# A decoder layer on one core: the order of steps on all five engines replaced, 19 products of zeros fewer

## The reference

```python
x = x + attn(layernorm(x), Wqkv, Wo)       # 16 heads of 16, rope, causal softmax
x = x + xattn(layernorm(x), ctx, ~mask)    # softmax(x @ ctx.T / 16) @ ctx, masked
x = x + ffn(layernorm(x), ...)
# ffn: probs = softmax(x @ gate_w.T); the 2 best of 8 experts, weights not renormalised
#      every expert is computed: h_e = silu(x @ w1_e.T) * (x @ w2_e.T), 176 wide
#      y = sum_e comb_e * (h_e @ w3_e.T) + the same form with a shared part, 352 wide
```

## Time and profile before

| what | value |
|---|---|
| median of 3 runs | 284.23 us (284.11 to 285.96) |
| the profiled execution's own time | 284.33 us |
| its span, from first to last instruction | 282.7 us |
| granted TensorE clock, mean | 0.998 |
| busy share of the span | PE 95%, PEld 75%, ACT 61%, DVE 59%, POOL 42% |

### The profile page before, as it was taken

How to read it: one execution, slowest core, us unless ns; L and a number is a source line. 1 busy time by engine, 2 the same in 40 slices (tenths; PEclk the granted TensorE clock), 3 DMA queues, 4 the chain that set the end, 5 groups by cost and what they waited for, 6 DMA issues and landing times.

```text
span 282.7 us, 4951 instructions
## 1 busy us (share of the span) xinstructions
PE 267.5 (95%) x1834; PEld 212.2 (75%) x1844; DVE 166.5 (59%) x361; ACT 172.6 (61%) x288; POOL 120.1 (42%) x133
## 2 busy tenths in 40 slices
...
GB/s 231 371 378 9 0 3 5 0 4 0 2 0 4 75 5 260 0 5 74 2 3 113 253 42 3 1 3 0 0 2 16 58 175 227 10 2 1 0 0 77
DMA packets 11879, 17.09 MB, mean 60 GB/s; under 512 B 1904, under 2 KB 8272, under 8 KB 11856
## 3 DMA queue, kind: packets, MB, share of 16 engines
...
...
## 4 chain that ended last, share of the span: by engine, by line
PE 69%; ACT 9%; POOL 9%; DMA 5%; issue 3%; DVE 2%; SPq 1%; DVEq 0%; ACTq 0%; POOLq 0%
PE bank L758 28%; PE bank L866 14%; PE bank L771 8%; PE bank L812 3%; PE bank L765 3%; DMA gate_raw<-gate 3%; PE bank L798 2%; PE bank L919 2%; POOL prob_lo L392 2%; DMA q_t<-negm_t 2%; PE bank L836 2%; POOL w_lo L399 2%; PE bank L791 2%; PE bank L816 2%; ACT q_t L493 2%
## 5 line engine op out<-in xcount | busy, mean ns | idle before, releaser
L392 POOL TENSOR_TENSOR prob_lo<-prob,prob_hi 128x1536 f16<-128x1536 f32 x16 | 49.7, 3118 | 22.7 <-ACT prob_hi L512 22.6
L758 PE MATMUL bank<-x_hi,w_hi 128*128 128x512 f32 x112 | 45.5, 407 | 0.3 <-ACT prob L505 0.3
L758 PE MATMUL bank<-x_hi,w_lo 128*128 128x512 f32 x112 | 44.2, 395 | 0.0
L758 PE MATMUL bank<-x_lo,w_hi 128*128 128x512 f32 x112 | 44.0, 393 | 0.0
L549 ACT CAST h_hi<-h_c 128x512 fp32r<-128x512 f32 x28 | 17.3, 620 | 41.8 <-DVE h_c L735 23.2
L726 DVE TENSOR_TENSOR h_c<-bank,h_s 128x512 f32<-128x512 f32 x28 | 19.3, 690 | 31.2 <-PE bank L758 21.6
L583 DVE TENSOR_REDUCE negm<-bank 128x2 f32<-128x512 f32 (+1 forms) x48 | 31.2, 684 | 6.8 <-PE bank L793 3.9
L866 PE MATMUL bank<-w_hi,h_hi 128*128 128x256 f32 x112 | 32.5, 290 | 0.1
L740 DVE TENSOR_TENSOR h_lo<-h_c,h_hi 128x512 fp32r<-128x512 f32 x28 | 20.2, 728 | 19.5 <-ACT h_hi L549 19.5
L866 PE MATMUL bank<-w_lo,h_hi 128*128 128x256 f32 x112 | 31.7, 283 | 0.0
L866 PE MATMUL bank<-w_hi,h_lo 128*128 128x256 f32 x112 | 31.6, 283 | 0.0
...
## 6 DMA issues: line engine op xcount, KB each, us to landing
...
```

The source lines that it names most:

```text
L392: eng.tensor_tensor(prob_lo[:, b % 2], prob[:, b % 2], prob_hi[:, b % 2], ALU.subtract)\
L758: ins = pe.matmul(dst, a(k), c(k), start=(k == 0 and i == 0), stop=(k == kt - 1 and i == 2))
```

## The change

The five lists of `ORDER` are replaced. SP, POOL, ACT and DVE keep exactly their steps (16, 73, 228 and 200) in another order. PE keeps its steps too, but for the products of zeros: `early` falls from 33 to 14, `late` stays at 19. Nothing else in the file changes; a blank line goes, so that the lines of the new kernel are one lower. The head and the tail of the lists, and the middle where `up.0` begins:

```diff
     "SP": """
-        ln1.0 mt.0 mt.1 mt.2 ro.0 w3.0 ct.0 mt.3 ro.1 ct.1 cb.0 ct.2 y.0 ct.3 cb.1 y.1
+        ln1.0 mt.0 mt.1 mt.2 w3.0 ct.0 mt.3 ro.0 ct.1 cb.0 ct.2 ro.1 ct.3 cb.1 y.0 y.1
     "POOL": """
-        ln1.0 ln1.1 tr.7 qk.0 ln1.2 sh.0 qk.1 ln1.3 w12.0 sh.1 w12.1 w12.2 w12.3 w12.4 w12.5 w12.6 qk.2 sh.2 qk.3
+        ln1.0 ln1.1 qk.0 sh.0 tr.7 qk.1 sh.1 ln1.2 w12.0 qk.2 sh.2 w12.1 qk.3 sh.3 qk.4 ln1.3 h.0 h.1 sh.4 h.2 qk.5
...
     "ACT": """
...
-        s.41 h.13 s.42 s.43 s.44 ln3n.1 t3.1 s.45 s.46 h.14 lg.1 s.47 h.15 up.0 ct.1 ot.2 dn.0 up.1 dn.1 w3.0 w3.1
+        w12.8 s.45 s.46 s.47 lg.1 h.14 up.0 ct.1 ot.2 h.15 dn.0 w12.9 up.1 ln2n.2 t2.2 w12.10 w3.0 up.2 xs.2 w3.1
...
     "PE": """
...
-        pv.13 late.1 up.0 ct.1 pv.14 ot.2 up.1 wo.2 pv.15 up.2 dn.0 dn.1 t2.2 up.3 xs.2 up.4 pt.2 up.5 ro.2 dn.2
+        late.1 s.43 late.6 s.44 s.45 late.3 t3.1 s.46 late.1 pv.12 lg.1 s.47 pv.13 up.0 ct.1 late.2 ot.2 late.1
+        pv.14 wo.2 up.1 up.2 t2.2 pv.15 xs.2 up.3 pt.2 dn.0 ro.2 dn.1 dn.2 up.4 up.5 t3.2 dn.3 up.6 lg.2 up.7
...
-        dn.24 dn.25 dn.26 dn.27
+        dn.18 dn.19 up.21 up.22 dn.20 dn.21 up.23 up.24 dn.22 dn.23 up.25 up.26 dn.24 up.27 dn.25 dn.26 dn.27
```

More of the change, by code:

```diff
@@ L59 @@
     """,
     "ACT": """
[L61 to L65, removed]
@@ L76 @@
[L76 to L80, removed]
@@ L81 @@
[L81 to L84, removed]
+        ln1.0 ln1.1 zero.0 qk.0 v.0 vm.0 qk.1 ln1.2 zero.1 kt.2 kt.3 v.1 qk.2 m.0 m.1 kt.6 m.2 m.3 kt.7 vm.1 m.4 m.5
@@ new lines @@
+        m.6 m.7 m.8 m.9 m.10 m.11 qk.3 kt.10 kt.11 qk.4 ln1.3 kt.14 kt.15 m.12 m.13 m.14 m.15 m.16 pv.0 m.17 m.18
+        m.19 m.20 m.21 m.22 m.23 qk.5 pv.1 pv.2 kt.18 kt.19 pv.3 on.0 v.2 kt.22 vm.2 kt.23 wo.0 ln2.0 m.24 m.25 m.26
+        m.27 m.28 qk.6 m.29 m.30 xs.0 m.31 qk.7 m.32 m.33 m.34 xc.0 m.35 pv.4 ro.0 ln3.0 pv.5 kt.26 pv.6 t3.0 kt.27
+        lg.0 rk.0 kt.30 kt.31 pv.7 m.36 m.37 on.1 m.38 m.39 m.40 m.41 m.42 pv.8 wo.1 ln2.1 m.43 m.44 m.45 m.46 m.47
+        v.3 pv.9 xs.1 vm.3 pv.10 pv.11 xc.1 ro.1 ln3.1 on.2 t3.1 pv.12 lg.1 rk.1 pv.13 up.0 wo.2 ln2.2 dn.0 pv.14
@@ L85 @@
+        up.1 xs.2 up.2 pv.15 dn.1 dn.2 xc.2 ro.2 up.3 ln3.2 up.4 dn.3 up.5 t3.2 dn.4 up.6 lg.2 rk.2 on.3 dn.5 up.7
+        dn.6 wo.3 dn.7 ln2.3 up.8 dn.8 up.9 up.10 xs.3 xc.3 dn.9 ro.3 ln3.3 dn.10 up.11 dn.11 up.12 t3.3 dn.12 up.13
+        lg.3 dn.13 up.14 rk.3 y.0 up.15 dn.14 dn.15 up.16 up.17 dn.16 up.18 dn.17 dn.18 up.19 dn.19 up.20 dn.20
+        up.21 dn.21 up.22 dn.22 up.23 dn.23 up.24 up.25 dn.24 up.26 dn.25 dn.26 up.27 dn.27 y.1
     """,
     "PE": """
-        xt.0 qk.0 v.0 qk.1 early.10 xt.1 tr.0 tr.1 qk.2 tr.2 tr.3 v.1 tr.4 tr.5 m.0 m.1 tr.6 m.2 tr.7 m.3 qk.3
@@ L88 @@
[L88 to L92, removed]
```

42 lines of the change are left out of this document (25 added, 17 removed).

## The result

The changed kernel takes **276.42 us** (median of 4 runs, 276.24 to 276.50) where the kernel before took 284.17 beside it (283.51 to 285.96). The ratio is 0.9717, with a 95% interval of 0.9672 to 0.9761. The profiled execution took 276.24 us and has a span of 274.7, so 8.0 us less than before. Single runs of several kernels of this document, of the kernel before too, have a lower mean granted clock (0.985 to 0.994) and take 1.3 to 3.5 us longer.

A forecast was written before the change was run, and what follows sets the result against it. Prediction: PE bounds behind `up.0`, a chain of hand-offs ahead of it. Terms -5.3 + 1.5 - 0.2 - 2.4 - 1.0 + 1.4 = -6.0, less 0.9 given back: -5.1 from 284.33, so 279.2 us, range 276.5 to 283.0.

The forecast's parts named there:

- stage 1: From the start to the first shift of the maxima on ACT, at 40.93 us before: predicted -5.3 us.
- stage 4: From the third to the fourth shift of the maxima: 28.0 us instead of 30.4, predicted -2.4 us.
- the discount of +0.9: Over the whole kernel, 0.9 us given back because not every hand-off followed would succeed at once; an estimate.
- the zeros: 19 fewer products of zeros on PE, 4.1 us: said to fill waits, credited nothing, wrong by 1 us at most.
- What bounds it: PE bounds behind the first feed-forward matmul (141.15 us); ahead of it a chain of hand-offs does, with no engine full.
- the walk: Following the new lists from post to post, with the old trace's durations and PE-to-reader distances; terms sum to -6.0 us.
- Stages 2 and 3: First to second shift, +1.5 us as moved-out work comes back; second to third shift, -0.2 us.
- Stage 5: From the fourth shift to the first feed-forward matmul, `up.0`: 19.5 us instead of 20.5, predicted -1.0 us.
- behind `up.0`: From the first feed-forward matmul to the end, 141.6 us before: predicted +1.4 us, mostly PE waiting for a low part.
- My posts: Predicted times of the four sequences' shifts of the maxima on ACT and of `up.0`, which divide the kernel into stages.
- The gain is given back by late low parts: Rival, chance 0.17: low parts coming 4 us later on POOL set the end of stages 3 and 4; 282.9 us.
- The clock falls: Rival, chance 0.08: with fewer zeros PE's clock halves among transposes and small products; 287.2 us with 8 us lost.

The follow-up runs named there:

- zeros_none: The changed kernel without any early or late products of zeros, only the 16 at the very start kept; 280.89 us, ratio 0.9888 to the kernel before.
- first_stage_clean: New orders up to about the sixth exp, the kernel before's behind, with weight casts and remainders moved later so `h.2` doesn't wait; 283.11 us, ratio 0.9959.

## Why the prediction was right in direction and short in size

Forecast 279.2, measured 276.42: the direction and the order of the gains by stage held, and the gain was 7.8 us, not 5.1, which is 0.1 us beyond the fast end of the range (276.5 to 283.0). The steps that failed are sizes in the sum: stage 1 with -5.3 where -6.3 was measured, stage 4 with -2.4 for -3.3, the discount of +0.9 where nothing had to be given back, and the zeros, put at nothing, which the runs price at 1.9 to 2.55 us. By the prediction's own steps:

- **What bounds it** held. Nothing is won where PE is full: `up.0` starts 9.0 us sooner, and 1.0 of it is lost behind.
- **Stage 1 was sized 1.0 us short.** The rope among the maxima was read right (3.0 us shown, 3.5 predicted with a share of waiting). The first maximum came 2.6 us sooner, not 1.8; the two small moves alone bring 0.7 and 1.0 of it. The maxima themselves took 10.6 us, 0.5 more than I had. From the end of the last to the shift it is 0.5 us, where I had carried along the old trace's 1.2: the walk overlooked that `qk.5` had stood ahead of `mt.0` on PE. So the miss is 0.8 - 0.5 + 0.7 us.
- **Stages 2 and 3** held within 0.5 us (+1.8 for +1.5, +0.3 for -0.2): what was moved out comes back. The later lists must take it in: with the old ones only 1.3 us of stage 1's gain is left.
- **Stage 4 was sized 0.9 us short**, though its mechanism was the strongest that the runs showed (4.2 us). `h.8` on ACT came at 98.30, where my walk had 98.7; some 0.7 us of the miss lie in the stretch behind it, to the fourth shift, which the walk had too long. Which distance there was too long is not shown.
- **Stage 5** was 0.6 us short, and **behind `up.0`** 0.4 too dear.
- **The zeros failed as a step.** I credited them nothing, since they filled waits of the old order, and bounded the error by 1 us. Put back into the new order they cost 1.9 us in the first three stages and 2.55 us in all. My posts had been walked with the new list, so part of that stood in the stages already and the sum did not lose all of it. But the claim that they only fill waits is wrong for this order: ten of them cost 1.3 us in the new stage 2 and nothing in the old one.
- **The discount of +0.9 went the wrong way.** The terms without it give 278.3. The walk was too slow in stages 1, 4 and 5 and behind `up.0`, too fast in 2 and 3. In stage 1 a distance copied from the old trace held a step that had moved away, so the walk had a reserve in it already, and the discount came on top.
- **The rivals.** "The gain is given back by late low parts": POOL's wait of 6.26 us became 2.13, so room was there. "The clock falls" did not happen to the changed kernel (0.998 to 1.0 in four runs) but does close by: with no zeros, with the rope among the maxima, and with fewer zeros in the old order. Where it lasted 3.4 us a stage became 1.1 to 1.7 us longer, where it lasted 6.8 us 1.2, and where it lasted 10.2 us 2.6, with 0.9 more behind `up.0`. I had 4 to 5 us for a stretch of 9 and 8 in all; zeros_none, with 13.7 us at half clock ahead of 138 us, took 4.5 us more. The Trainium skill (TensorE: Matmul & The Clock Gate, Part 4: PE-mode transpose) says that transposes don't count as a busy PE in the same way. Five of the seven falls agree, as they begin among transposes or just behind them (19.3, 19.5, 35.6, 39.3 and 120.8 us). One begins among scores, between waits of 1.4 and 0.7 us (127.7), and one inside a wait of 6.3 us with no transpose near (59.5), so transposes are not needed for a fall. Whether they bring one without waits is not shown.

What stays open: why the clock falls in some runs of a kernel and not in others of the same one; how much of the earlier first maximum the two small moves bring together; how the 2.2 us that stage 2 of first_stage_clean loses against the changed kernel part between `s.5` and `v.2`; and whether zeros lengthen the landing of the third shift's DMA.
